# A GNN step waits for its own gathered chunk, counted by SyncE and loaded by TensorE, instead of for the newest chunk

## The reference

```python
q = (x @ qw + qb).reshape(N, H, D)
k = (x @ kw + kb).reshape(N, H, D)
v = (x @ vw + vb).reshape(N, H, D)
alpha = jnp.einsum('ehd,ehd->eh', q[dst], k[src]) * scale
m = jax.ops.segment_max(alpha, dst, num_segments=N)
ex = jnp.exp(alpha - m[dst])
denom = jax.ops.segment_sum(ex, dst, num_segments=N)
w = ex / (denom[dst] + 1e-16)
agg = jax.ops.segment_sum(w[:, :, None] * v[src], dst, num_segments=N)
return agg.mean(axis=1) + x @ sw + sb      # layer 2 takes h = this + x @ lin1_w + lin1_b
```

## Time and profile before

| | |
|---|---|
| median of 3 runs | 1221.49 us (1221.37 to 1224.63) |
| profiled execution | 1220.84 us, its span 1219.0 us |
| busy share of the span | PE 82%, DVE 81%, ACT 64%, POOL 62% |
| gathers issued | 5.8 to 500.9 us (layer 0), 610.8 to 1103.4 us (layer 1) |
| steps' first halves | 38.7 to 534 us and 615.5 to 1137 us |
| granted TensorE clock, mean | 0.94 of full speed |

### The profile page before, as it was taken

How to read it: one execution, slowest core, us unless ns; L and a number is a source line. 1 busy time by engine, 2 the same in 40 slices (tenths; PEclk the granted TensorE clock), 3 DMA queues, 4 the chain that set the end, 5 groups by cost and what they waited for, 6 DMA issues and landing times.

```text
span 1219.0 us, 32111 instructions
## 1 busy us (share of the span) xinstructions
PE 1002.1 (82%) x6792; PEld 778.5 (64%) x6792; DVE 984.2 (81%) x5260; ACT 785.4 (64%) x2594; POOL 756.6 (62%) x804
## 2 busy tenths in 40 slices
PE   4778888888797889888986787879788978898887
PEld 3546667767575667677753565657576757676775
DVE  5798989888787888899487777777877878888976
ACT  1356767777575769676274364758575758678755
POOL 7777777777777777300077777777777777771000
PEclk9988999999999989999897799999998989999988
DMA  5323333333322333100133332323332323230001
GB/s 141 88 76 89 89 80 89 82 86 79 80 79 80 79 80 81 45 2 1 53 103 79 80 80 70 87 73 85 78 81 72 86 73 88 71 88 26 2 2 53
DMA packets 51941, 87.04 MB, mean 71 GB/s; under 512 B 16699, under 2 KB 25169, under 8 KB 51761
## 3 DMA queue, kind: packets, MB, share of 16 engines
q0 software_dynamic: 25024, 51.30, 16.7%
q1 hardware_dynamic: 24145, 32.62, 9.2%
q10 hardware_dynamic: 2592, 1.07, 0.4%
HBM read 81.58 MB, written 3.34 MB: 70 GB/s over the span
## 4 chain that ended last, share of the span: by engine, by line
PE 27%; POOL 18%; issue 18%; DVE 17%; DMA 13%; ACT 4%; DVEq 2%; SPq 0%; POOLq 0%; ACTq 0%
POOL gathered L424 18%; PE ps L703 14%; DMA gathered<-h_rows,src_e 8%; PE ps L691 7%; DVE junk L980 5%; DVE acc L1011 5%; DMA gathered<-in_x,src_e 5%; ACT whot L525 4%; PE ps L802 2%; PE ps L797 1%; PE ps L786 1%; DVE apart L991 1%; DVE max_b L1049 1%; DVEq L285 1%; DVEq L1011 1%
## 5 line engine op out<-in xcount | busy, mean ns | idle before, releaser
L703 PE MATMUL ps<-gathered,whot 128*128 x3328 | 573.3, 300 | 86.6 <-ACT whot L525 64.4
L525 ACT ACTIVATE whot<-apart,below 128x128 f32<-128x128 bf16 x1664 | 551.5, 388 | 124.3 <-DVE apart L991 108.8
L703 PEld LDWEIGHTS ps<-gathered,whot 128*128 128x128 f32 x3328 | 457.5, 200 | 167.3 <-issue 128.5
L980 DVE SCALAR_TENSOR_TENSOR junk<-ps,gathered 128x129 f32<-128x129 f32 x1664 | 413.3, 286 | 149.0 <-issue 76.4
L691 PE MATMUL ps<-table,hot_t 128*128 x2496 | 443.4, 287 | 62.9 <-DVE junk L980 40.9
L424 POOL DMA_INDIRECT gathered<-in_x,src_e x391 | 377.1, 965 | 119.7 <-issue 75.6
L424 POOL DMA_INDIRECT gathered<-h_rows,src_e x391 | 374.7, 958 | 118.9 <-issue 74.4
L1011 DVE TENSOR_TENSOR acc<-ps,acc 128x258 f32 x832 | 350.7, 421 | 19.3 <-PE ps L703 9.8
L691 PEld LDWEIGHTS ps<-table,hot_t 128*128 128x128 bf16 x2496 | 251.0, 101 | 154.6 <-issue 110.0
L509 ACT ACTIVATE apart<-col_b,ndl_e 128x128 bf16<-128x128 bf16 x618 | 239.2, 387 | 0.0
L980 DVE DVE_READ_ACCUMULATOR junk<-ps,gathered 128x1 f32 x1664 | 135.8, 82 | 0.3
(11 more groups left out here) (176 smaller groups left out, 554.0 us busy)
## 6 DMA issues: line engine op xcount, KB each, us to landing
dl_bc<-local_dst_rows SPq DMA_DIRECT2D x104, 256.0 KB
gathered<-in_x,src_e POOLq DMA_INDIRECT x391
gathered<-h_rows,src_e POOLq DMA_INDIRECT x391
h_rows<-table SPq DMA_DIRECT2D x6, 256.0 KB, 2.3
out<-x_rows SPq DMA_DIRECT2D x6, 256.0 KB
table<-in_L_gnn_q_w ACTq DMA_DIRECT2D x2, 128.0 KB
table<-in_L_gnn_k_w ACTq DMA_DIRECT2D x2, 128.0 KB
wv<-in_L_gnn_v_w ACTq DMA_DIRECT2D x2, 128.0 KB
```

Source lines behind the costliest of these rows:

```text
L525: last = nc.scalar.activation(whot[:, c % UN, h, :], apart[:, c % UN, :], ACT.Exp, scale=FAR, bias=below[:, j % 2, h, o:o + 1])
L703: last = nc.tensor.matmul(bank_u[n % NB][:, h * C1:(h + 1) * C1], whot[:, c % UN, h, :], gathered[:, bass.ds(slot, 1), :].rearrange("p o c ...
L980: last = V.scalar_tensor_tensor(out=junk[:, t % 2, h, :], in0=bank_t[n % NB][:, h * C1:(h + 1) * C1], scalar=1.0, in1=gathered[:, bass.ds( ...
```

## The change

- A semaphore `landed[l]` for each layer counts the chunks that have landed, in order: SP waits for one chunk's `got` after the other and adds one each time.
- A row of pairs `tile_i` holds for each step its bin and the number of chunks up to its own (the chunk's number, at most 390, plus one). Two small DVE operations make it at the start.
- PE loads pairs in place of bins, 16 values for eight steps, and takes each count through an AND with 511. `step_t` on PE waits for `landed[l]` to reach its step's count.
- The wait for `got` in `step_alpha` on DVE goes. The ring's wait on POOL stays as it was.
- The broadcasts into `dl_bc` move from SP to ACT: the first two stay on SP, the others are issued by ACT at each eighth slot (`spread_ahead`), two broadcasts ahead. SP stores the later rows of destinations (`store_rows`) once it has counted eight chunks.

```diff
+        def tiles_of(etype, step):
+            _, v = nc.values_load_multi_w_load_instructions(
+                tile_i[0:1, step:step + RB, :].rearrange("o s v -> o (s v)"), engines=[etype], min_val=0, max_val=CHUNKS,
...
+            return [(v[2 * k].with_bounds(min_val=0, max_val=BINS - 1), (v[2 * k + 1] & 511).with_bounds(min_val=1, max_val=CHUNKS)) for k in range(RB)]
...
+        def spread_rows(eng, n):
+            q = n % per_layer
+            eng.dma_start(dl_bc[:, n % 2, :], dl_flat[:, q * BC * P:(q + 1) * BC * P].to_broadcast([P, BC * P])
+                          ).then_inc(dl_in[n % 2], 16)
...
+            sp.wait_ge(rows_out[0], 16 * G)
+            for n in range(2):
+                spread_rows(sp, n)
             for l in range(2):
-                for q in range(per_layer):
-                    n = l * per_layer + q
-                    if l == 0 and q == 2:
+                for c in range(CHUNKS):
+                    n = l * CHUNKS + c
+                    if l == 0 and c == EARLY_CHUNKS:
                         for w in range(1, ROW_SETS):
                             store_rows(w)
-                    if n >= 2:
-                        sp.wait_ge(S["hot_t_ready"], n - 1)
...
-                    sp.dma_start(dl_bc[:, n % 2, :],
...
+                    sp.wait_ge(got[n % GQ], 16 * (n // GQ + 1))
+                    sp.sem_inc(landed[l], 1)
...
+            def spread_ahead(l, a):
+                n = l * per_layer + a // BC + 2
+                if n < 2 * per_layer:
+                    act.wait_ge(S["hot_t_ready"], n - 1)
...
+                    spread_rows(act, n)
...
+                    if a is not None and a % BC == 0:
+                        spread_ahead(l, a)
...
-            def step_t(l, t, b):
+            def step_t(l, t, b, count):
...
                 if n >= NB:
                     pe.wait_ge(S["alpha_ready"], n - NB + 1)
+                pe.wait_ge(landed[l], count)
...
-                                b = bins_of(PE, 0)
+                                b = tiles_of(PE, 0)
...
-                            step_t(l, k, b[k % RB])
+                            step_t(l, k, *b[k % RB])
...
+            V.tensor_tensor(tile_i[:, :, 0], step_f[0:1], bank_r[64:65, 0:STEPS], ALU.subtract)
+            V.tensor_scalar(tile_i[:, :, 1], bank_r[64:65, 0:STEPS], float(CHUNKS - 1), 1.0, ALU.min, ALU.add)
...
             def step_alpha(l, t, slot):
-                m = l * CHUNKS + newest(t)
...
-                if t == newest(t):
-                    dve.wait_ge(got[m % GQ], 16 * (m // GQ + 1))
                 dve.wait_ge(S["t_ready"], n + 1)
```

More of the change, by code:

```diff
@@ L55 @@
 LATE_ROWS, LATE_DST, LATE_MASKS = 1, 6, 7
+EARLY_CHUNKS = 8
 NGR = -(-BINS // G)
@@ L175, in program @@
         bin_i = sb("bin_i", [1, STEPS], i32)
+        tile_i = sb("tile_i", [1, STEPS, 2], i32)
         slot_i = sb("slot_i", [1, STEPS], i32)
@@ L250, in program @@
         dl_in = [sem(f"dl_in{k}") for k in range(2)]
+        landed = [sem(f"landed{l}") for l in range(2)]
         banks = [bank_s, bank_r]
@@ L281, in bins_of @@
             return v
+        def tiles_of(etype, step):
+            _, v = nc.values_load_multi_w_load_instructions(
+                tile_i[0:1, step:step + RB, :].rearrange("o s v -> o (s v)"), engines=[etype], min_val=0, max_val=CHUNKS,
+                skip_runtime_bounds_check_because="a step's tile of nodes, within 0..24 by the staircase, and the number of "
+                                                  "chunks up to its own, 1..CHUNKS")
+            return [(v[2 * k].with_bounds(min_val=0, max_val=BINS - 1), (v[2 * k + 1] & 511).with_bounds(min_val=1, max_val=CHUNKS)) for k in range(RB)]
         def slots_of(etype, step):
@@ L288, in slots_of @@
             return v
-        def newest(t):
-            return min(t, CHUNKS - 1)
         def slots():
@@ L320, in made @@
             return l * by_dve.count(dve) + by_dve[:c + 1].count(dve)
+        dl_flat = dl_d.rearrange("(o s) e -> o (s e)", o=1)
+        per_layer = STEPS // BC
+        def spread_rows(eng, n):
+            q = n % per_layer
+            eng.dma_start(dl_bc[:, n % 2, :], dl_flat[:, q * BC * P:(q + 1) * BC * P].to_broadcast([P, BC * P])
+                          ).then_inc(dl_in[n % 2], 16)
         @block.sync
@@ L351, in _ @@
             store_rows(0)
-            dl_flat = dl_d.rearrange("(o s) e -> o (s e)", o=1)
-            per_layer = STEPS // BC
+            sp.wait_ge(rows_out[0], 16 * G)
+            for n in range(2):
+                spread_rows(sp, n)
             for l in range(2):
-                for q in range(per_layer):
-                    n = l * per_layer + q
-                    if l == 0 and q == 2:
+                for c in range(CHUNKS):
+                    n = l * CHUNKS + c
+                    if l == 0 and c == EARLY_CHUNKS:
                         for w in range(1, ROW_SETS):
                             store_rows(w)
-                    if n >= 2:
-                        sp.wait_ge(S["hot_t_ready"], n - 1)
-                    w = BLOCK_OF[(q + 1) * BC - 1] // G
-                    if l == 0 and (q == 0 or w != BLOCK_OF[q * BC - 1] // G):
-                        sp.wait_ge(rows_out[w], 16 * len(range(G * w, min(G * (w + 1), NBLK))))
-                    sp.dma_start(dl_bc[:, n % 2, :],
-                                 dl_flat[:, q * BC * P:(q + 1) * BC * P].to_broadcast([P, BC * P])
-                                 ).then_inc(dl_in[n % 2], 16)
+                    sp.wait_ge(got[n % GQ], 16 * (n // GQ + 1))
+                    sp.sem_inc(landed[l], 1)
                 if l == 0:
@@ L503, in scan @@
                                    ).then_inc(S["below_ready"], 1)
+            def spread_ahead(l, a):
+                n = l * per_layer + a // BC + 2
+                if n < 2 * per_layer:
+                    act.wait_ge(S["hot_t_ready"], n - 1)
+                    if l == 0 and n < per_layer:
+                        w = BLOCK_OF[(n + 1) * BC - 1] // G
+                        if w != BLOCK_OF[n * BC - 1] // G:
+                            act.wait_ge(rows_out[w], 16 * len(range(G * w, min(G * (w + 1), NBLK))))
+                    spread_rows(act, n)
             def far_apart(l, c):
@@ L754, in _ @@
                             if k % RB == RB - LOAD_AHEAD and k + LOAD_AHEAD < STEPS:
-                                b_next = bins_of(PE, k + LOAD_AHEAD)
+                                b_next = tiles_of(PE, k + LOAD_AHEAD)
                             if k < BINS:
                                 pe.wait_ge(S["part3"], l * BINS + k + 1)
-                            step_t(l, k, b[k % RB])
+                            step_t(l, k, *b[k % RB])
                     if s is not None:
```

## The result

The changed kernel takes 1190.88 us (median, 1188.98 to 1193.69), beside 1223.01 us for the kernel before: a ratio of 0.9739, interval 0.9713 to 0.9765. It is 2.6% faster, 32 us. The forecast was 1190 us.

The account below looks back on a forecast made before the run. Gathers were taken to pace layer 0 from step 192 and most of layer 1. Layer 0 -9.5, layer 1 -23.3 and tails +1 give -31.8 us off the 1221.49 us median: 1190 us, range 1170 to 1226 us.

Parts of the forecast that it names:

- The gain: Steps wait for their own chunk, not the newest: 23 us in layer 0, 25 in layer 1, 48 us before costs.
- free pace of the steps in layer 0: From step 192 steps run unheld by gathers, 53.5 us a block of 48, reaching step 344 at 424.5 us.
- landing of the right chunk up to step 344 in layer 1: Gathers still bound layer 1 to step 344, whose chunk 327 lands only at 1027 us; free pace would give 1008.
- The cost: Added work, mainly on PE's sequencer: 12.5 + 1 us in layer 0, 1.7 in layer 1, 1 in the tails.
- the AND: On PE's sequencer, AND and register wait together add one instruction a step, 0.12 us, between bounds 0 and 0.24.
- the longer load: PE's load of 16 values, not 8, adds 0.03 us a step, between bounds 0 and 0.07.
- two servers at 0.90 and 0.92, coupled by three PSUM buffers: PE's sequencer at 0.90 us a step and VectorE at 0.92 lose time to each other, 0.035 us a step.
- Rival D: As C, and the 16-value load costs two of 8 or the register wait 0.05 us more: 1242 us, chance 0.18.
- C: Wait and AND are one instruction each on PE's sequencer, which bounds at 1.02 us a step: 1212 us, chance 0.18.
- one microsecond: While a layer is at bin 0, SP's count before PE's matmuls delays work about 1 us once, not every step.
- SyncE's count, ScalarE's broadcasts, VectorE's two operations: Count: about 1 us once a layer; broadcasts: 47 us of issues on ACT, taken as 0; VectorE's startup operations: 1 us.
- idle time on PE: Sign of failure: the prediction is wrong if VectorE idles on PE rather than on gathers; no size given.

Follow-up runs that it names:

- e7_dve_const: Kernel before, with VectorE's wait on the step's own chunk written in as constants, nothing else: 1174.07 us against 1222.33 us, ratio 0.9597.
- e2_const: Changed kernel with each step's count a constant, loads of 8 bins and no AND: 1177.83 us, ratio 0.9620 to the kernel before.
- e5_count_only: Changed kernel loading only the counts, 8 values for eight steps, with the bin worked out in the address: 1177.15 us, ratio 0.9634 to the kernel before.
- e1_newest: Changed kernel with the count loaded for each step that of the newest chunk, all else kept: 1229.15 us, ratio 1.0054 to the kernel before.

## Why the prediction came out

**The gain.** Predicted 48 us, measured 48.3 us with own chunks alone. By layer, to the last addition: 23 and 25 us predicted; 22.3 us (572.9 to 550.6) and 24.7 us (603.4 to 578.7) in e7_dve_const. The two limits that I worked with were right: free pace of the steps in layer 0, landing of the right chunk up to step 344 in layer 1.

**The cost.** Predicted 16 us, measured 17 us (0.9739 against 0.9597). The sum is right, its parts are not, and that they made up the same sum is in part luck. I gave 0.12 us a step to the AND and 0.03 us to the longer load, and made both one load on the sequencer's mean. The AND took 0.092 us, and together with all else but the long load it cost 4.5 us (3.4 us of uncertainty); the load took 0.514 us more, 0.064 us a step, near the end of the range (two loads of 8), and cost 13 us. In a step without a scan the loss was 0.02 us (23.1 and 22.5 us for the same 25 steps), and I had taken 0.035; it stood within the 0.93 to 0.98 us that I had named. What was wrong is "two servers at 0.90 and 0.92, coupled by three PSUM buffers": the mean of 0.91 us (0.75 + 0.092 + 0.064) was about what I had, but 77 us of the sequencer's time spread over all steps as ANDs are inside those 4.5 us, and 53 us in 104 pieces cost 13 us. My reading is that a tenth of a microsecond in each step is bridged by what PE's queue and the PSUM buffers hold, and 1.1 us in one piece is not. The split load bears that out in a 1646 us set; in the 1222 us set it is argued, since the mean near VectorE's pace wasn't ruled out there. Rival D's condition, the load of two, came true without its price, since the wait on a register was free and C's two instructions a step were one.

The Trainium skill's 600 ns (DMA: Bandwidth & Descriptors, Latency and other measured facts) agrees with the 590 ns of 8 values, but it is no floor that 16 values stay at: they took 1105 ns, and 24 took 1617. The 200 ns that the Trainium skill (Runtime: NRT & Kernel Launch, Instruction fetch mechanics) gives for a register loaded from HBM don't hold for these loads from SBUF: each value beyond the eighth took 64 ns.

**Where the cost fell.** In layer 0 step 192 came at 263.3 us instead of 255.1 us; I had 6.5 us for it. In e2_const it came at 254.7 us, in e5_count_only at 257.5 us and in e7_dve_const at 258.3 us: single profiles differ by some 3 us here, and the AND has no share that shows. The clock has none either: from 38 to 255 us it was granted at 0.94 both before and after. From there to step 392 the changed kernel took 5.4 us more than e7_dve_const, with 7 us predicted. In layer 1 it lost 5.0 us against 2.2 us predicted (1.7 and the tail). Three of the five fall before step 64, with bin 0 and each step on its landing, where I had let one microsecond pass. What they are isn't shown: against e7_dve_const, e2_const loses 1.0 us there, e5_count_only 1.9 us, and e1_newest, which has the long load too, 1.5 us, all in single profiles. Step 392 of layer 1 started at 1083.3 us; I had named 1090 less layer 0's shift of 10 us.

**SyncE's count, ScalarE's broadcasts, VectorE's two operations.** Hidden as forecast, as far as e2_const can tell (2.8 us, with 3 us of uncertainty); an issue on ScalarE took 0.326 us and not 0.45. VectorE was busy 206.53 of 230 us (90%) from 255 to 485 us, and 410.63 of 500 us (82%) from 590 to 1090 us, where I had named 84%. Its idle time on PE did appear, which I had named as a sign of failure: 53.2 us of waits for L717, 35.0 us before. It is no such sign: e5_count_only has 56.4 us of it. It is what VectorE waits for once the gathers don't hold it.

**The ring.** One effect I had not named: in layer 0 the last gather started at 505.3 us instead of 500.9, and GpSimd waited up to 1.9 us for a slot that PE's second halves free, 0.3 us before. It goes with the long load: e1_newest, which has it, ends at 504.7 us, and e2_const, e5_count_only and e7_dve_const end at 501.2 to 501.5 us. It cost nothing that shows: behind step 192 of layer 0 PE waited for landings 4.1 us in all, and 4.7 us in e2_const.

## What to carry to other kernels

Ask of every wait whether it names what the instruction reads or a bound on it; where a stream of transfers paces a stage, a wait for a later item costs its distance times the pace, and only there. Price an addition to a sequencer by its longest single stand as well as by its mean: ninety nanoseconds in every step vanished within the uncertainty, half a microsecond in every eighth cost 13 us. When two values can be worked out from each other, load one into a register and compute the other.

## What the runs showed of the hardware

**Register loads grow by the value.** 8 values 0.590 us, 16 values 1.105 us, 24 values 1.617 us: 64 ns each, on some 77 ns for the rest.

**Instructions of PE's sequencer take longer than they are shown with.** In the changed kernel's trace the next one starts 124 ns after an address operation (shown with 46 ns), 106 ns after a wait (51 ns), 92 ns after the AND (32 ns) and 647 ns after a load of 8 values (591 ns), each as the commonest or shortest distance.

**A wait on a register's value is as cheap as one on a constant.** It rode on an address operation; the same wait on a constant, in e2_const, stood by itself, 51 ns as the trace shows it.

**The 1646 us sets.** There VectorE's products (286 ns) and the gathers (944 ns in the median) are as long as in the 1222 us set, and the mean granted clock is 0.84 in place of 0.94. The trace of e7_dve_const from such a set, 40 to 120 us (stream kinds with packets, MB and share), and then the same kernel in the 1222 us set:

```profile
q0 software_dynamic: 2048, 4.20, 20.1%
q1 hardware_dynamic: 494, 0.56, 2.3%
```

```profile
q0 software_dynamic: 1962, 4.04, 19.8%
q1 hardware_dynamic: 1629, 2.43, 10.6%
q8 instruction: 4, 0.07, 0.3%
q14 instruction: 5, 0.04, 0.2%
```

In the 1646 us set no instruction transfer took place in these 80 us, while the gathers went on at their pace; all eight traces of the two sets show this. In this time PE stood still for 84.7 us at L639, and VectorE and ScalarE for 87 us each. The waits, and then the end of PE's stand and the last gather before the ring was full:

```profile
POOL gathered L426 <- PE ps L705: 422.2, 208, 118.3
PEld ps L693 <- issue: 283.5, 237, 16.4
...
PEld ps L639 <- issue: 88.5, 3, 84.7
DVE table L889 <- issue: 87.0, 1, 87.0
ACT table L460 <- issue: 86.8, 1, 86.8
```

```profile
122.09 0.50 PEld L639 LDWEIGHTS ps<-table 128*128 128x128 f32 x2 [84.74 <-issue]
127.29 0.94 POOL L426 DMA_INDIRECT gathered<-in_x,src_e  x1 [0.31 <-issue]
```

At the start of layer 1 PE did a few matmuls at a time with some 14 us between (starts at 864.52, 879.92, 896.08, 912.85 and 929.68 us), until the ring was full again (last gather at 968.1 us). One could think that the gathers keep the instruction transfers from being served there. But PE's long stand ended 5 us before the gathers paused, and the first instruction transfers after it came only at 144.6 and 149.1 us, so no instruction transfer shows at its end. No experiment tested it, and what PE waited for, and why two sets do this and the third not, stays open. What the waits do show is that in these sets GpSimd waits for PE, so the gathers are not the bound; that fits with own chunks gaining nothing there.
